# Reordering the terms of the routed down product, with a wait for each term

## The reference

```
gate = ragged_dot(xs, w_gate, group_sizes)
up = ragged_dot(xs, w_up, group_sizes)
down = ragged_dot(silu(gate) * up, w_down, group_sizes)
routed = (down[unsort].reshape(T, K, H) * tkw[..., None]).sum(axis=1)
```

## Time and profile before

| | us |
|---|---|
| median of 3 runs (11729.92 to 11731.9) | 11729.98 |
| time of the profiled execution | 11792.17 |
| span in its trace | 11790.5 |
| TensorE busy | 11326.4 |
| VectorE busy | 4600.6 |
| GpSimd busy | 4274.9 |
| ScalarE busy | 2987.6 |
| the expert stage in the trace, gate of the first tile to down of the last | 2949 to 11751 |

### The profile page before, as it was taken

One profiled execution on the slowest core, in us unless ns is written; L12 is line 12 of the kernel. 1 busy time (PEld: TensorE's weight loads), 2 busy tenths in 40 slices (PEclk: granted clock), 3 DMA queues, 4 the chain that ended last, 5 costly groups with the idle time before them and its releaser, 6 DMA issues.

```text
span 11790.5 us, 200734 instructions
## 1 busy us (share of the span) xinstructions
PE 11326.4 (96%) x50496; PEld 9288.4 (79%) x50497; DVE 4600.6 (39%) x6239; ACT 2987.6 (25%) x4098; POOL 4274.9 (36%) x4236
## 2 busy tenths in 40 slices
PE   8999779998999999999999999999999999999998
PEld 7877557776888888888888878878887787888887
DVE  5666566664323323333323233232334323223222
ACT  2111144442222222222222222222223222222221
POOL 2555442221333333333333333333333333333333
PEclk9999889999999999999999999999999999999999
DMA  4333266765444444444544454454555545444443
GB/s 157 127 130 125 93 172 175 181 178 151 101 107 106 117 96 117 117 121 113 138 96 117 96 148 104 97 134 96 138 130 169 138 97 152 97 96 117 97 96 84
DMA packets 918209, 1451.51 MB, mean 123 GB/s; under 512 B 314531, under 2 KB 585059, under 8 KB 895049
## 3 DMA queue, kind: packets, MB, share of 16 engines
q0 software_dynamic: 212800, 623.06, 24.7%
q10 hardware_dynamic: 384512, 383.85, 11.6%
q1 hardware_dynamic: 320776, 443.28, 11.4%
HBM read 853.67 MB, written 596.15 MB: 123 GB/s over the span
## 4 chain that ended last, share of the span: by engine, by line
PE 66%; DVE 2%; issue 2%; DMA 2%; ACT 1%; DVEq 1%; ACTq 0%; POOL 0%; SPq 0%; POOLq 0%
PE pd L66 7%; PE pd L68 7%; PE pd L67 7%; PE pg L66 7%; PE pg L68 7%; PE pg L67 7%; PE pu L68 7%; PE pu L67 7%; PE pu L66 7%; DMA activated<-av 1%; DVE w_lo L1908 1%; DMA aq<-activated 1%; ACT w_hi L1817 1%; DVEq L1589 0%; DVE aT L1931 0%
## 5 line engine op out<-in xcount | busy, mean ns | idle before, releaser
L1772 POOL DMA_INDIRECT xq<-xn_rows,idx_q x2124 | 2187.0, 1030 | 936.6 <-issue 486.9
L1780 POOL DMA_INDIRECT out_rows<-y,idx_s x528 | 864.3, 1637 | 4510.0 <-issue 4499.4
L1956 DVE SCALAR_TENSOR_TENSOR av<-pu,scale,sg 128x512 f32<-128x512 f32 x528 | 396.3, 751 | 3610.0 <-PE pu L68 3397.4
L66 PE MATMUL pd<-w_hi,a_hi 128*128 128x512 f32 x4224 | 1661.7, 393 | 122.1 <-DVE a_lo L1935 89.6
L66 PE MATMUL pg<-w_hi,x_hi 128*128 128x512 f32 x4224 | 1645.3, 390 | 47.3 <-DVE x_lo L1924 39.4
L67 PE MATMUL pd<-w_lo,a_hi 128*128 128x512 f32 x4224 | 1654.1, 392 | 0.0
L68 PE MATMUL pd<-w_hi,a_lo 128*128 128x512 f32 x4224 | 1653.6, 391 | 0.0
L66 PE MATMUL pu<-w_hi,x_hi 128*128 128x512 f32 x4224 | 1644.8, 389 | 4.9 <-DVEq L1973 4.8
L67 PE MATMUL pg<-w_lo,x_hi 128*128 128x512 f32 x4224 | 1644.6, 389 | 0.0
L68 PE MATMUL pg<-w_hi,x_lo 128*128 128x512 f32 x4224 | 1644.4, 389 | 0.0
L67 PE MATMUL pu<-w_lo,x_hi 128*128 128x512 f32 x4224 | 1643.6, 389 | 0.0
(11 more groups left out here) (286 smaller groups left out, 14552.6 us busy)
## 6 DMA issues: line engine op xcount, KB each, us to landing
stage<-in_w_all SPq DMA_DIRECT2D x174, 1024.0 KB, 15.1
activated<-av ACTq DMA_DIRECT2D x528, 256.0 KB
aq<-activated ACTq DMA_DIRECT2D x528, 256.0 KB
rep<-steps ACTq DMA_DIRECT2D x192, 512.0 KB
xq<-xn_rows,idx_q POOLq DMA_INDIRECT x2124
xt<-in_x SPq DMA_DIRECT2D x64, 512.0 KB
xn_rows<-xn SPq DMA_DIRECT2D x64, 512.0 KB, 2.6
xn_turned<-sx_hi SPq DMA_DIRECT2D x64, 512.0 KB
```

The lines of the kernel that those rows point to most:

```text
L66: m(dst, hi, whi[:, cols], start=begin, stop=False)
L1772: g.indirect_dma_start(out=xq[q][:, n], out_offset=None, in_=xn_q, in_offset=bass.IndirectOffsetOnAxis(ap=idx_q[q][:, n:n + 1], axis=0))\
L1780: g.indirect_dma_start(out=out, out_offset=bass.IndirectOffsetOnAxis(ap=idx_s[q][:, 0:1], axis=0), in_=y[q][:], in_offset=None, compute_op ...
L1956: v.scalar_tensor_tensor(out=av[:], in0=pu[:], scalar=scale[q][:].bitcast(F32), in1=sg[:], op0=ALU.mult, op1=ALU.mult).then_inc(av_ready, 1)
```

## The change

`down(t)` no longer calls `down_half`. For each half it issues all four high x high products, then the four with the low weights, then the four with the low activations. The three kinds have a wait each, in the first half only: `ah_ready` before the first kind, `down_weights` before the second, `al_ready` before the third. The wait on `y_ready` comes first now. The number of matmuls, their operands and the increment of `down_done` at the end of each half stay.

```diff
@@ -1991,11 +1991,17 @@
         @block.tensor
         def _(pe):
             def down(t):
-                pe.wait_ge(al_ready, t + 1)
-                pe.wait_ge(down_weights, t + 1)
                 wait_past(pe, y_ready, t * 2)
                 for h in range(2):
-                    down_half(nc, pd[h][:], a_hi, a_lo, w_hi, w_lo, h).then_inc(down_done, 1)
+                    parts = ((a_hi, w_hi, ah_ready), (a_hi, w_lo, down_weights), (a_lo, w_hi, al_ready))
+                    for n, (rows, weights, ready) in enumerate(parts):
+                        if h == 0:
+                            pe.wait_ge(ready, t + 1)
+                        for i in range(KI):
+                            c = i % 2 * H + h * 512
+                            last = nc.tensor.matmul(pd[h][:], rows[:, i], weights[4 + i // 2][:, c:c + 512],
+                                                    start=n == 0 and i == 0, stop=n == 2 and i == KI - 1)
+                    last.then_inc(down_done, 1)
```

## The result

The changed kernel takes 11706.56 us (median of 18 runs), the kernel before 11731.48 us (median of 18): 24.9 us less, a ratio of 0.9978 with a 95% interval of 0.9972 to 0.9985. The forecast was 11703 us, with a range of 11688 to 11724.

A forecast was written before the change was run, and what follows sets the result against it. The prediction took TensorE, busy 96% of the span, as the bound. Terms of 16.7, 10.0 and 2.8 us made 29.5, lowered to 27 for unprofiled runs: 11730 - 27 = 11703 us, range 11688 to 11724.

The forecast's parts named there:

- The wait: First down matmul of a waiting tile: starts 0.14 us after a_hi instead of a_lo, 0.725 us earlier; al_ready costs nothing.
- Passed on within a run of late tiles: Consecutive waiting tiles: of 31 follow-up waits 10 pass nothing, 21 pass between 0.06 and 0.725 us; 10.0 us in total.
- the link: Second eviction on ScalarE, between two waiting tiles: can start 0.67 us earlier and no more, held by the load of aq.
- The waits in all: TensorE before the first down matmul: 54 waits or a few less, released by a_hi, about 95 us instead of 122.1.
- The clock: TensorE after three late starts of 1.95 to 2.0 us: slow bursts vanish, which passes on 2.8 us.
- The sum: Profiled execution: 16.7 us kept by 22 runs and the last tile, 10.0 passed on, clock 2.8; together 29.5 us.
- The step from the profiled execution to the median: Unprofiled runs are 62 us shorter, place unknown; waits may be shorter there, so the gain is taken as 27 us.
- The slow rival: Satisfied waits inside the down product delay the next weight load: 11809 us at 0.1 us each, 11956 at 0.24; chance 0.05.
- the one by which nothing is passed on: Between waiting tiles nothing is passed on: gain only 16.7 us; rival range 11713 to 11722 us, chance 0.27.
- Its other half: Waits before down clearly shorter in unprofiled runs: gain some 8 us if half are too short; shares the chance 0.27.
- the change does nothing: Late down starts are released by down_weights or y_ready, so the time stays at 11730 us; chance 0.02.
- everything is kept: All 54 late down starts keep 0.725 us and the three clock drops go in full: 44 us, 11686 us; chance 0.04.

The follow-up runs named there:

- experiment 1: The changed kernel with all three waits put back ahead of the down product, new order of products kept: 11730.43 us, ratio 0.9999 to the kernel before.
- experiment 2: The changed kernel with down_weights waited for up front, high-activation products interleaved as of old, one inner wait for al_ready: 11705.41 us, ratio 0.9978 to the kernel before.
- experiment 4: The kernel before with one more, unused operation of a_lo's size on VectorE between a_hi and a_lo: 11779.03 us, ratio 1.0041 to the kernel before.
- experiment 5: The changed kernel with one more, unused operation of a_lo's size on VectorE between a_hi and a_lo: 11702.34 us, ratio 0.9976 to the kernel before.
- experiment 3: The changed kernel with 19 more long-satisfied waits per tile in gate, up and down: 11705.75 us, ratio 0.9977 to the kernel before.

## Why the prediction was right, point by point

**The wait.** A late down product starts 0.14 to 0.15 us behind `a_hi`, and `a_lo` ends 0.58 us after the start in nearly all of them: together the 0.725 us of the sum. Experiments 1 and 2 show that this wait alone carries the gain, and 4 and 5 that the eight matmuls ahead of the third kind cover the time that `a_lo` still needs.

**Passed on within a run of late tiles.** In the pair of the earlier trace rows I had given the link 0.67 us of room. ScalarE and TensorE in the new trace:

```profile
3514.19 0.33 ACTq L1832 DMA_DIRECT2D aq<-activated  x1
3514.46 1.06 ACT L1844 ACTIVATE y<-pd 128x512 f32<-128x512 f32 x2
3517.30 3.73 ACT L1817 ACTIVATE w_hi<-stage 128x2048 fp32r<-128x2048 f32 x2 [1.78 <-issue]
...
3525.95 1.16 PE L2002 MATMUL pd<-w_hi,a_hi 128*128 128x512 f32 x4 [0.62 <-ACT a_hi L1837]
```

From the end of `a_hi` to the split it was 9.32 us before and is 3517.30 - 3508.61 = 8.69: 0.63 us were passed on. (The prediction's sign for this, a split that starts sooner after the down product's first start, named the wrong point to measure from: that start itself comes sooner, and from it to the split it is 8.54 us now and was 8.43.)

Over all 53 late starts ahead of the very last tile, the traces of experiment 1 and of the changed kernel can be compared tile by tile. The 22 that begin a run of late tiles gained 16.0 us in all, and 22 x 0.725 is 16.0. The 31 that follow another late tile gained 11.8 us; 10.0 were forecast. Single starts scatter from 1.2 us lost to 1.4 us gained, so the exact fit of the first sum is luck; against the trace of the kernel before the two sums are 18.1 and 12.0 us.

**The waits in all.** Expected were 95 us of idle time left and 54 waits or a few less; there are 91.3 us and 46. By the distance to the matmul before, 51 down products still start late; the shortest waits fall below what the view counts.

**The clock.** This term is not borne out. The three late starts that had a slow burst are 1.0 to 1.3 us late now, and these bursts are gone; two of the three:

```profile
5657.00:5662.40 5.40, 5.34 (x24) 1.00 0.98 196
6347.30:6352.70 5.40, 5.35 (x24) 1.00 0.98 201
```

Each of the two windows has 24 matmuls again, where the slow window of the earlier trace rows had 17. But the 2.8 us that the sum took for it don't show in the stage as a whole: 121 of its matmuls follow each other at 0.4 to 0.5 us now, against 127 in the trace before and 116 in experiment 1, whose waits are those of the kernel before. Some of the bursts behind waits of 3 us and more are longer now. And how many there are changes from one execution to the next: behind late starts of about 2.0 us experiment 1 has one, the kernel before three.

**The sum.** 29.5 us for the profiled execution stands against 31.1 between the two stages, and against 24.2 if the stage of experiment 1 is taken for the kernel before. The medians say 24.9, so the comparison with experiment 1 is the typical one, and the sum was some 5 us too large for it. The profiled execution before had a few longer waits (122.1 us against 119.8) and more time at the low clock (96 us of the stage after its first tiles against 89, idle time included). Ahead of the down products 28.1 us went (119.8 to 91.7). The clock brought nothing. And a term that the prediction put at nothing took part of the gain back, the waits ahead of gate and up. In experiment 1:

```profile
PE pg L66 <- issue: 7.7, 2, 6.4
...
PE pu L66 <- DVEq L1973: 4.1, 6, 1.1
```

In the changed kernel:

```profile
PE pg L66 <- issue: 10.0, 6, 6.4
...
PE pu L66 <- DVEq L1973: 6.0, 7, 1.0
```

Together 11.8 us have become 16.0, and 28.1 - 4.2 = 23.9 is the 24.2 us but for 0.3. It is no chance of one execution: experiments 2, 3 and 5, which wait for `a_hi` too, have 17.1, 16.6 and 16.2 us, and the trace before 12.7. The new waits stand in runs of late tiles. In the changed kernel every late start of gate comes 0.45 us and every one of up 0.40 us behind the end of a low part of the weights (L1908): TensorE comes sooner now and finds the split still going. This is read from the trace; no experiment tests it.

**The step from the profiled execution to the median was wrong in its reason.** I said the profile doesn't say where its 62 us more lie, and took 2.5 us off because they might be in the waits. The trace after says it: some 52 to 57 us lie ahead of the expert stage, in stages that the change does not touch. The deduction was small and happened to point the right way. That 27 us came so close to the 24.9 measured is in part luck: the clock's 2.8 us and the 4.2 us of new waits were too much, and the 1.8 us more that was passed on and these 2.5 us offset a good part of them. The largest terms, the 16.7 us and the 10.0, hold by themselves.

**The rivals.** The slow rival is refuted (experiment 3). So is the one by which nothing is passed on: the follow-up starts gained 11.8 us, and 16.7 us in all lies just outside the interval of the gain, 18 to 33 us. Its other half, that the waits are clearly shorter in a typical run, fails as well: the profiled execution of experiment 1 took 11732.9 us, 2.4 us above its median, and had 54 waits of 119.8 us. That the change does nothing, and that everything is kept (44 us), both lie outside the interval. The rule of the Trainium skill ("TensorE: Matmul & The Clock Gate", Part 2) that weights can be loaded once for many matmuls makes no difference here: the order alone measures 0.9999, and there are 50497 weight loads for 50496 matmuls before and after.

## What to carry to other kernels

A product of split factors can wait for each of its parts where that part is first used; order the terms so that what is made last is used last, and count how many matmuls cover it. Look first at whether the wait is a real one and in how many tiles: here it was in 54 of 528, and the gain is 54 times one small operation (39 us), less what the next waits take back, ahead of the same product and ahead of others: 25 us are left. Then ask what the released wait hangs on: moving one transpose ahead of 4.5 us of splitting was worth twice as much as the reordering.

## What the runs showed of the hardware

- Waits on satisfied semaphores between matmuls of 512 columns cost nothing measurable: 10032 more of them moved the median by 0.8 us.
- A late start of TensorE of about 2.0 us was followed by the lower clock in 3 of 5 cases in the kernel before and, with those up to 2.7 us, in 16 of 29 in experiment 4; shorter ones never were, in either. Between the profiled stages of experiments 1 and 4, 0.64 us more of waiting in 54 places made 58 us and not 35; between the medians it is 47 to 49 us. The Trainium skill ("TensorE: Matmul & The Clock Gate", "Why this matters for your kernels") advises to have no idle gaps of over some 3 us between bursts of matmuls; in these traces that is not strict enough.
